# Sorting edges on one core: ranks by comparison within a lane and sums over lanes, instead of a scan over the flags

## What is computed

```python
# x [6250, 256]; src, dst [106250]; edge_weight [106250]
xn = layernorm(x)
support = xn @ W                        # 256 x 256
r = sigmoid(support @ a2)
msg = (r * support)[dst] * edge_weight[:, None]
out = segment_sum(msg, src, 6250) / segment_sum(edge_weight * r[dst], src, 6250)[:, None]
l = softplus(out @ a1)
x = x + elu(max(out, 0) + l * min(out, 0))
# then a slice attention block with 8 heads and 64 slices on layernorm(x), added to x
```

## Time and profile before

| | |
|---|---|
| median of three runs | 1511.26 us |
| the profiled execution | 1511.66 us |
| its span | 1509.8 us |
| busy in the span: PE, DVE, POOL, ACT | 1222.1, 1089.0, 900.1, 371.7 us |
| mean granted clock of TensorE | 0.912 of full |
| start up to the gating of rows | 0 to 36 us |
| gating, sort of groups 1 to 5 | 36 to 196 us |
| sort of groups 6 to 25, first 294 tiles | 196 to 641 us |
| main gather, attention's sums beside it | 641 to 1420 us |
| product with the last weights, output | 1420 to 1510 us |

### The profile page before, as it was taken

One profiled execution on the slowest core, in us unless ns is written; L12 is line 12 of the kernel. 1 busy time (PEld: TensorE's weight loads), 2 busy tenths in 40 slices (PEclk: granted clock), 3 DMA queues, 4 the chain that ended last, 5 costly groups with the idle time before them and its releaser, 6 DMA issues.

```text
span 1509.8 us, 21274 instructions
## 1 busy us (share of the span) xinstructions
PE 1222.1 (81%) x6061; PEld 901.0 (60%) x6061; DVE 1089.0 (72%) x2846; ACT 371.7 (25%) x1174; POOL 900.1 (60%) x920
## 2 busy tenths in 40 slices
PE   4577668777888878668898888888888888888998
PEld 3466567776777767434565555555544555555787
DVE  9856899999999999235777676767667676664322
ACT  1343201111111001001333332323333333333232
POOL 0000177777777777767777777777777777770000
PEclk9989878888999989878899998999999999998999
DMA  8111144456555555556444446444444444441022
GB/s 258 38 52 51 42 62 129 130 132 144 146 143 138 138 136 150 136 109 121 113 115 113 112 115 118 116 114 112 116 112 116 116 111 114 113 112 44 22 76 73
DMA packets 158693, 166.46 MB, mean 110 GB/s; under 512 B 84303, under 2 KB 129251, under 8 KB 158588
## 3 DMA queue, kind: packets, MB, share of 16 engines
q0 software_dynamic: 42848, 114.59, 28.8%
q1 hardware_dynamic: 94572, 31.24, 9.0%
q10 hardware_dynamic: 21168, 19.35, 4.2%
HBM read 136.73 MB, written 28.38 MB: 109 GB/s over the span
## 4 chain that ended last, share of the span: by engine, by line
DVE 24%; PE 23%; POOL 22%; issue 16%; DMA 11%; POOLq 2%; ACT 2%; SPq 0%; DVEq 0%; ACTq 0%
PE bank L1599 22%; POOL rows L781 18%; DMA rows<-gated_rows_dram,ring_i 9%; DVE big L869 7%; POOL rows L700 3%; DVE S L1055 3%; DVE big L882 3%; DVE big L909 3%; POOLq L773 2%; DMA sorted_edges_dram<-big,idx 1%; DVE big L896 1%; DVE big L856 1%; DVE big L878 1%; ACT rows L1439 1%; DVE big L891 1%
## 5 line engine op out<-in xcount | busy, mean ns | idle before, releaser
L1599 PE MATMUL bank<-rows,S 128*128 128x257 f32 (+1 forms) x2254 | 642.2, 410 | 139.8 <-DMA rows<-gated_rows_dram,ring_i 102.0
L781 POOL DMA_INDIRECT rows<-gated_rows_dram,ring_i x564 | 541.8, 961 | 178.0 <-issue 158.9
L1599 PEld LDWEIGHTS bank<-rows,S 128*128 128x128 f32 x2254 | 413.4, 199 | 325.7 <-DMA rows<-gated_rows_dram,ring_i 192.6
L700 POOL DMA_INDIRECT rows<-gated_rows_dram,lg x294 | 298.4, 1015 | 95.7 <-issue 76.2
L1599 PE MATMUL bank<-big 128*98 128x80 f32 (+2 forms) x1741 | 196.6, 280 | 72.8 <-DVE big L909 70.4
L1599 PEld LDWEIGHTS bank<-big 128*98 128x98 f32 (+1 forms) x1741 | 192.1, 197 | 84.7 <-issue 82.5
L1223 DVE TENSOR_SCALAR S<-iota,lof,srec 128x128 f32<-128x128 f32 x637 | 178.0, 351 | 3.7 <-PE bank L1599 3.6
L688 POOL DMA_INDIRECT sorted_edges_dram<-big,idx x52 | 59.0, 1134 | 186.9 <-ACT big L1412 122.4
L1234 DVE TENSOR_TENSOR ag<-bank,ovr 128x257 f32<-128x257 f32 x49 | 20.9, 427 | 191.9 <-PE bank L1599 191.9
L1458 ACT COPY ovr<-bank 128x257 f32<-128x257 f32 x98 | 36.7, 374 | 334.7 <-PE bank L1599 322.0
L1599 PE MATMUL bank<-Wxs,xT 128*128 128x512 f32 x196 | 115.6, 720 | 0.1
(11 more groups left out here) (239 smaller groups left out, 1339.2 us busy)
## 6 DMA issues: line engine op xcount, KB each, us to landing
overflow_sums_dram<-ovr ACTq DMA_DIRECT2D x98, 128.5 KB
rows<-gated_rows_dram,ring_i POOLq DMA_INDIRECT x564, 2.8
gated_rows_dram<-rows SPq DMA_DIRECT2D x49, 128.5 KB, 2.7
ovr<-overflow_sums_dram SPq DMA_DIRECT2D x49, 128.5 KB, 2.3
out_dram<-S SPq DMA_DIRECT2D x48, 128.0 KB, 1.7
rows<-gated_rows_dram,lg POOLq DMA_INDIRECT x294, 3.1
res<-in_x_dram SPq DMA_DIRECT2D x1, 4352.0 KB
xn<-overflow_sums_dram ACTq DMA_DIRECT2D x33, 128.5 KB, 3.0
```

Of the source, the lines that this page charges most:

```text
L700: pool.indirect_dma_start(rows[:, turn(n), :], None, gtab[:, :], bass.IndirectOffsetOnAxis(ap=ring1[:, n:n + 1], axis=0)).then_inc(s_row[t ...
L781: pool.indirect_dma_start(rows[:, slot(b, u), :], None, gtab[:, :], bass.IndirectOffsetOnAxis(ap=ring_i[:, b // CH % 2, n:n + 1], axis=0)) ...
L1599: return nc.tensor.matmul(o, l, r, start=start, stop=stop, skip_group_check=True)
```

## The change

The rank of an edge is now the sum over its own lane and the lanes above (`lowerb` compares with `is_ge`, so that `above` includes the edge's lane) less the number of edges of the same bucket and half that come later in its own lane. So the scan goes:

- `lookup(g)` (DVE, L888) multiplies the flags with the sums of their bucket, one value for 16 columns, and takes the place of the scan and L896. The flags lose their column 0; ACT copies the sums into a small table `base2`, with each sum twice, for which `above` has 196 columns instead of 98 and reads `folded` with a step of 16 elements.
- `later(g)` (DVE, L880 and L882): compares all pairs of columns of a half (16 x 2 x 16 = 512), and multiplies with a triangle of -1. Its 16 rows stand behind the 49 of `prod`, and `quads` adds them up too: 65 x 32 = 2080 columns instead of 49 x 32 = 1568.
- `spread_flags(g)` (DVE, L864): the flags again, [lane, column, bucket], which `values` (L872) then reads without a step. From group 7 on its bucket numbers, and `later`'s triangle, are in PSUM.
- `counts` goes: `total` takes the last lane of `base2` with a column that is 1 in lane 127.

```diff
-            v.memset(reset, 1.0)
-            step(v.memset(oneb, 1.0))
-            v.memset(halved(reset)[:, :, :, 0:1], 0.0)
-            v.tensor_scalar(lowerb, iota[:, :], iotap[:, 0:1], None, ALU.is_gt)
+            v.tensor_scalar(lowerb, iota[:, :], iotap[:, 0:1], None, ALU.is_ge)
+            v.tensor_scalar(lastb, iotap[:, :].broadcast_to([P, 2]), float(P - 1), None, ALU.is_equal)
+            step(v.tensor_tensor(tri, iotab[:, 0:HC].unsqueeze(2).broadcast_to([P, HC, HC]),
+                                 iotab[:, 0:HC].unsqueeze(1).broadcast_to([P, HC, HC]), ALU.is_gt))
+            v.tensor_scalar(tri, tri, -1.0, None, ALU.mult)
...
+            def spread_flags(g):
+                b = iota2 if g > G1 + 1 else iotab[:, 0:NB]
+                step(v.tensor_tensor(flagsj, hib[:, g * GC:(g + 1) * GC].unsqueeze(2).broadcast_to([P, GC, NB]),
+                                     b.unsqueeze(1).broadcast_to([P, GC, NB]), ALU.is_equal))
             def values(g, h):
...
-                                        flags4[k][:, :, h, 1:HS].rearrange("p b j -> p j b"),
+                                        flagsj[:, h * HC:(h + 1) * HC, :],
...
+            def later(g):
+                hb = hib[:, g * GC:(g + 1) * GC].rearrange("p (h j) -> p h j", h=2)
+                t = tri2 if g > G1 + 1 else tri
+                step(v.tensor_tensor(same, hb.unsqueeze(1).broadcast_to([P, HC, 2, HC]),
+                                     hb.rearrange("p h i -> p i h").unsqueeze(3).broadcast_to([P, HC, 2, HC]), ALU.is_equal))
+                v.tensor_tensor(prod[:, NB * GC:(NB + HC) * GC].rearrange("p (i h j) -> p i h j", h=2, j=HC), same,
+                                t.unsqueeze(2).broadcast_to([P, HC, 2, HC]), ALU.mult)
+
+            def lookup(g):
                 k = g % 2
                 dve.wait_ge(s_bs, g + 1)
-                    step(v.tensor_tensor_scan(run, reset, flags[k], 0.0, ALU.mult, ALU.add))
...
+                v.tensor_tensor(halved(prod[:, 0:NB * GC], HC), flags4[k],
+                                base2[k][:, :, 0, :].rearrange("p h b -> p b h").unsqueeze(3).broadcast_to([P, NB, 2, HC]),
+                                ALU.mult).then_inc(s_prod, 1)
...
-                ranks(g)
+                lookup(g)
                 pair(g, 0)
-                counts(g)
...
+                spread_flags(g)
                 values(g, 0)
...
                 quad(g)
+                if g + 1 < NG:
+                    later(g + 1)
                 hot(g, 0)
...
-                a.copy(flags4[k][:, :, :, 0], bank[0][:, 0:2 * NB].rearrange("p (b h) -> p b h", h=2)).then_inc(s_bs, 1)
+                a.copy(base2[k].rearrange("p h v b -> p (h v b)"), bank[0][:, 0:4 * NB]).then_inc(s_bs, 1)
...
-                    m = mm(bank[0][:, 0:VB], lowerb, folded[k][:, :, :, j], j == 0, j == HC // 2 - 1)
+                    m = mm(bank[0][:, 0:4 * NB], lowerb, folded[k][:, :, :, j].rearrange("p b h -> p h b").unsqueeze(2).broadcast_to([P, 2, 2, NB]), j == 0, j == HC // 2 - 1)
...
-                for n in range(0, NB * GC, wide):
+                for n in range(0, (NB + HC) * GC, wide):
```

More of the change, by code:

```diff
@@ L58 @@
 NG = EC // GC
-HS = HC + 1
 VB = 2 * NB
@@ L185, in build, with halved @@
         hot_v = [carve(HC * VB).rearrange("p (j v b) -> p j v b", v=2, b=NB) for k in range(2)]
-        def halved(t, j=HS):
+        def halved(t, j):
             return t.rearrange("p (b h j) -> p b h j", h=2, j=j)
-        flags = [carve(NB * HS, BF16) for k in range(2)]
-        flags4 = [halved(t) for t in flags]
-        folded = [carve(NB * HC // 2, BF16).rearrange("p (b h j) -> p b h j", h=2, j=HC // 2) for k in range(2)]
-        reset = carve(NB * HS, BF16)
-        run = carve(NB * HS, BF16)
-        run4 = halved(run)
-        reset2 = bank[3][:, 0:25 * HS]
+        flags4 = [halved(carve(NB * HC, BF16), HC) for k in range(2)]
+        flagsj = carve(NB * HC, BF16).rearrange("p (n b) -> p n b", b=NB)
+        folded = [halved(carve(NB * HC // 2, BF16), HC // 2) for k in range(2)]
+        base2 = [carve(2 * NB, BF16).rearrange("p (h v b) -> p h v b", h=2, b=NB) for k in range(2)]
+        same = carve(HC * GC // 2, BF16).rearrange("p (i h j) -> p i h j", h=2, j=HC)
+        tri = carve(HC * HC // 2, BF16).rearrange("p (i j) -> p i j", j=HC)
+        tri2 = bank[3][:, 0:HC * HC].rearrange("p (i j) -> p i j", j=HC)
+        iota2 = bank[4][:, 3 * GC:3 * GC + NB]
         vals2 = bank[4][:, 0:2 * GC].rearrange("p (v j) -> p v j", j=GC)
@@ L198, in build @@
         buckets = halved(carve(NB * HC, BF16), HC)
-        prod = carve(NB * HC, BF16)
-        cntp = [carve(2 * NB, BF16).rearrange("p (h v b) -> p h v b", h=2, v=2) for k in range(2)]
+        prod = carve((NB + HC) * HC, BF16)
         runs = [carve(2 * RUN)[0:VB, :] for k in range(2)]
@@ L855, in flag @@
                     dve.wait_ge(s_base, g - 1)
-                step(v.tensor_tensor(flags4[k][:, :, :, 1:HS],
+                step(v.tensor_tensor(flags4[k],
                                      hib[:, g * GC:(g + 1) * GC].rearrange("p (h j) -> p h j", h=2).unsqueeze(1)
@@ L875, in ranks @@
+            def lookup(g):
                 k = g % 2
                 dve.wait_ge(s_bs, g + 1)
-                if g <= G1 + 1:
-                    step(v.tensor_tensor_scan(run, reset, flags[k], 0.0, ALU.mult, ALU.add))
-                else:
-                    for lo in range(0, 2 * NB, 25):
-                        n = min(25, 2 * NB - lo) * HS
-                        m = v.tensor_tensor_scan(run[:, lo * HS:lo * HS + n], reset2[:, 0:n], flags[k][:, lo * HS:lo * HS + n],
-                                                 0.0, ALU.mult, ALU.add)
-                    step(m)
@@ L886, in counts @@
-            def counts(g):
-                k = g % 2
-                if g >= 2:
-                    dve.wait_ge(s_tot, g)
-                for h in range(2):
-                    m = v.tensor_tensor(cntp[k][:, h, :, :],
-                                        run4[:, :, h, HC:HS].rearrange("p b o -> p o b").broadcast_to([P, 2, NB]),
-                                        flags4[k][:, :, h, 0:1].rearrange("p b o -> p o b").broadcast_to([P, 2, NB]),
-                                        ALU.subtract)
-                m.then_inc(s_cp, 1)
-                v.tensor_tensor(halved(prod, HC), run4[:, :, :, 1:HS], flags4[k][:, :, :, 1:HS], ALU.mult).then_inc(s_prod, 1)
+                v.tensor_tensor(halved(prod[:, 0:NB * GC], HC), flags4[k],
+                                base2[k][:, :, 0, :].rearrange("p h b -> p b h").unsqueeze(3).broadcast_to([P, NB, 2, HC]),
+                                ALU.mult).then_inc(s_prod, 1)
@@ L951, in _ @@
             flag(1)
-            ranks(0)
-            counts(0)
+            later(0)
+            lookup(0)
             centre()
+            spread_flags(0)
             for h in range(2):
@@ L957, in _ @@
             quad(0)
+            later(1)
             for h in range(2):
@@ L1063, in _ @@
                     decode1(0, CH * KA, 0)
-                    step(v.tensor_copy(reset2, reset[:, 0:25 * HS]))
-                ranks(g)
+                    v.tensor_copy(iota2, iota[:, 0:NB])
+                    step(v.tensor_copy(tri2, tri))
+                lookup(g)
                 pair(g, 0)
-                counts(g)
                 if g + 1 < NG:
@@ L1616, in quads @@
                 wide = o.shape[-1]
[L1617 to L1619 removed]
+                for n in range(0, (NB + HC) * GC, wide):
+                    w = min(wide, (NB + HC) * GC - n)
+                    m = mm(o[:, 0:w], identb, prod[:, n:n + w], n == 0, n + wide >= (NB + HC) * GC)
                 m.then_inc(s_quad, 1)
@@ L1632, in add @@
             def add(lo, hi, k, h):
-                return mm(bank[2][0:VB, lo:hi], cntp[k][:, h, :, :].rearrange("p v b -> p (v b)"),
-                          oneb[:, lo:hi], False, False)
+                return mm(bank[2][0:VB, lo:hi], base2[k][:, h, :, :].rearrange("p v b -> p (v b)"),
+                          lastb[:, lo:hi], False, False)
             def total(g):
```

16 lines of the change are left out of this document (6 added, 10 removed).

## The result

The changed kernel took 1539.97 us (median of 4 runs, 1536.96 to 1541.3), beside 1511.66 for the kernel before (4 runs): ratio 1.0177, 95% interval 1.0153 to 1.0200. It is slower by 28.3 us; the direction was forecast, the size was not: 1523, range 1505 to 1533. The profiled execution took 1540.08 us (span 1538.2), the one of before 1511.66 (span 1509.8): 28.4 us between them.

What follows compares the result with a forecast made beforehand. POOL's unbroken row of indirect DMAs was taken as the bound, DVE savings worth nothing there. Start -0.35, group 6 -2.4, holds in groups 7 to 25 +15.2, wait -0.8: +11.7 on 1511.66, so 1523 us, range 1505 to 1533.

Steps and rivals of the forecast that it cites:

- `above` by column: PE's eight `above` matmuls, 98 to 196 columns: price taken to double with the columns, +1.56 us.
- L903 at the start: Before POOL's first fetch: this DVE product, L909 in the kernel before, starts at 31.9 us, not 29.87, +2.0.
- group 6: Group where everything still reads SBUF: POOL's over-time falls from 9.4 to about 7.0 us, -2.4 (ends -5 and +1).
- the wait at 355: POOL's one gap made by another engine, at 355 us: it goes, -0.8 us.
- the hold does not grow: Rival on POOL's DMAs: look-up runs packed or its length doesn't matter, 1507 us; chance 0.15.
- priced by instruction: Rival: the hold does not grow and `above` costs by instruction, another 7.5 us off, 1499; chance 0.05.
- DVE sets the pace: Rival: DVE, not POOL, sets the pace after all, 57 us saved, 1455; chance 0.03.
- PE takes the bound: Rival: POOL waits for PE 1 us in each of 7 groups up to 13, 1530 us; chance 0.06.
- two-input instructions hold nothing: Rival: POOL's long DMAs are long by chance; only -0.35 and -0.8 are left, 1510.5 us; chance 0.02.
- the clock before the first fetch: Group 1: PE's idle time goes and it stays at 2.4 GHz, -4.5 us, within that group's -6.3.
- Groups 2 to 4: Before POOL's first fetch: longer `above` and `quads`, +1.7 each; in all +5.7 for groups 2 and 3, +1.75 for 4.
- the hold of groups 7 to 25: DVE's two-SBUF-input instructions hold POOL's DMAs 0.8 us more a group, 19 x 0.8 = +15.2; ends 0.05 and 1.2 a group.

Runs made afterwards that it cites:

- e7b: Changed kernel with L864's flags written a second time in each group from 7 on, 34 us more DVE work: 1545.88 us, ratio 1.0213.
- e4b: Changed kernel with the look-up of groups from 1 on reading its sums from PSUM instead of SBUF: 1509.72 us, ratio 0.9978.
- e1c: Kernel before with only `above` made 196 columns wide, every sum written twice: 1523.12 us, ratio 1.0072.
- e2b: Changed kernel with `above` back at 98 columns, ACT's copy writing each sum twice: 1527.06 us, ratio 1.0104.
- e3c: Changed kernel with a DVE wait between look-up L888 and the first flags' look-up L855: 1534.28 us, ratio 1.0139.
- e2: Same kernel as e2b (changed kernel, `above` at 98 columns), run where the kernel before takes 1728 to 1735 us; first fetch 197.3 us, time not given.
- e7: Same kernel as e7b (changed kernel, L864's flags written twice from group 7 on), run where the kernel before takes 1728 to 1735 us; time not given.
- a0: The changed kernel run again, unchanged: 1543.72 us, ratio 1.0202 to the kernel before.
- e4: Same kernel as e4b (changed kernel, look-up from PSUM), run where the kernel before takes 1728 to 1735 us: 1754 us.
- e3: Same kernel as e3c (changed kernel, wait between the two look-ups), run where the kernel before takes 1728 to 1735 us: 1743 us.

## Why the prediction was wrong

**What held.** The kernel came out slower, as forecast, and by the two things that were looked for, `above` and the holds. POOL's row of DMAs is the bound: its gaps stayed 0.30, DVE has room (e7b), and the time went to the end through the last fetch. Held DMAs come of two SBUF inputs (e4b). The durations of every new instruction, `above` by column, L903 at the start (31.42 us, forecast 31.9 from 29.87) and group 6 (-3.8, forecast -2.4) came out near, and the wait at 355 went. In both of these places the terms as written do not add to what was taken: 1.4 + 0.2 + 0.69 + 0.45 is 2.7 and not 2.0 (measured 1.55), and group 6's terms leave 7.6 and not 7.0 (measured 5.6). The rivals fell: *the hold does not grow* (it grew), *priced by instruction* (374 ns), *DVE sets the pace* (e7b), *PE takes the bound* (gaps 0.30), *two-input instructions hold nothing* (e4b).

**First failed step: the clock before the first fetch.** Group 1 had the line "If the idle time goes, I take it that it stays at 2.4 GHz: (1 - 0.57) x 10.34 = -4.5". The idle time went, and the clock fell all the same. I read the earlier trace rows as an idle TensorE being granted less; the low clock followed `above` as well as the idle time, and one stretch couldn't tell the two. Nor was there so much to get: the two slow products of group 1 were 3.4 us over, not 4.5. Groups 2 to 4 were priced by length alone, +1.7 each, with no clock in them. What was measured: slow products are 11.7 us over instead of 3.4, so +8.3 where -4.5 stood, 12.8 us off, as much as this line missed (12.0). 1.1 of the 8.3 is the slow product in group 0, which no wide product precedes closely. e1c shows slow products with nothing but the width changed, 4.7 us of them; e2b takes 7.7 away again.

**Second failed step: the hold of groups 7 to 25,** "the growth is 0.8 to 0.85, I take 0.8: 19 x 0.8 = +15.2". Measured on the sum's own scale (over 1.25 a DMA, without the wait at 355): 15.4 before, 38.4 after, 23.0 in 19 groups, 1.2 a group. The step took it that a DMA slips through between the look-up and the flags, as it did before between L896 and L856. In 17 of the 19 groups it doesn't: the block that holds is L888 and L855 in one, 2.67 us long, which by the same count holds 2.67 - 0.63 = 2.0 where 1.15 + 0.35 were put down. e3c, with a gap, gets 5 to 8 us back. The upper end written beside the step, 1.2 a group, is what was measured; but it was put down to bad phases and not to this.

The sum by what was measured: 11.6 - 3.8 + 22.2 - 1.6 = 28.4.

**What stays open.** Why the clock falls behind `above`: its matmuls read one value every 32 bytes and take 374 ns for 196 columns (in e1c every 16 bytes, 367 ns), and the runs show that the width of this product brings slow products, not which property of it does. Why a DMA slips between L896 and L856, which overlap by 0.09 us, and not between L888 and L855, which overlap by 0.08: in the pair that lets it through the first instruction does 1.5 elements a ns (1568 in 1.02 us), in those that don't 0.9 (L888) or 0.5 (the two L869 of the earlier trace rows); no run here changed the rate alone. It can't be all, since L888 and L855 did let a DMA through in groups 6 and 7, and in e2 and e7 in 4 and 5 of the 19 groups from 6 to 24. Why some slow products remain with the narrow one, and why one stands in group 0.

## What to carry to other kernels

Where POOL issues indirect DMAs without a pause, count VectorE's instructions with two SBUF inputs, not its busy time: put one input into PSUM (here where the sums stood anyway, 34 us), and look whether such instructions stand back to back. A matmul's price is not its duration alone: look at the same later products before and after it, since here 7 us of length on `above` came with 5 to 8 us more on later products by the clock; duplicate a result on the engine that copies it out, not in the matmul. An instruction moved to win time at the start may lose it in the steady part, so read both parts.

## What the runs showed that was not expected

- Products that take 1.98 us take up to 3.77 for one or two pairs behind a train of eight 128x196 matmuls of 374 ns each, though TensorE was not idle ahead of it (4.15 us busy of 6).
- A gap of 0.03 to 0.04 us between two VectorE instructions lets a waiting DMA of POOL through (in every group of e3c where one waited); with an overlap of 0.08 it waited through both in 17 groups of 19.
- The same kernel takes 1512 us in some runs and 1728 to 1735 in others, once each way on what the record calls the same chip. A change need not show in both: the look-up from PSUM took 34 us off in the first (e4b against a0), and in the second e4 is not below e3 or e2.
